# GpSimd takes over the last multiplication of the first feed-forward kind, two tiles behind its clamps

## The reference, cut to what matters

```python
cw = jnp.sum(jax.nn.one_hot(idx, E) * weights[..., None], axis=1)   # top 2 of 8 experts, per token
h1 = jnp.einsum('td,efd->etf', xt, w1) + b1[:, None, :]
h3 = jnp.einsum('td,efd->etf', xt, w3) + b3[:, None, :]
a = swiglu(h1 * h3)        # g = min(h[::2], 7), l = clip(h[1::2], -7, 7); g * sigmoid(1.702 g) * (l + 1)
y = jnp.einsum('etf,edf->etd', a, w2) + b2[:, None, :]
routed = jnp.einsum('te,etd->td', cw, y)
sh = swiglu((xt @ sw1.T + sb1) * (xt @ sw3.T + sb3))
return (routed + sh @ sw2.T + sb2).reshape(inp_shape)
```

## Time and profile before

| What | us |
|---|---|
| median of 3 runs | 1880.45 (1879.37 to 1882.93) |
| the profiled execution | 1880.12 |
| its span (first to last instruction) | 1877.9 |
| PE busy | 1719.7 (92% of the span) |
| DVE busy | 1387.3 (74%) |
| ACT busy | 906.7 (48%) |
| POOL busy | 950.4 (51%) |

### The profile page before, as it was taken

The page is one execution under the profiler, slowest core; times in us unless marked ns, Lnnn a source line. Parts: engine busy times, 40 slices in busy tenths (PEclk is TensorE's granted clock), DMA queues, the critical chain, the costliest instruction groups (busy, mean ns, idle before and its releaser), DMA issues. The chain is left out here.

```text
span 1877.9 us, 23760 instructions
## 1 busy us (share of the span) xinstructions
PE 1719.7 (92%) x7374; PEld 936.2 (50%) x7381; DVE 1387.3 (74%) x2189; ACT 906.7 (48%) x2131; POOL 950.4 (51%) x986
## 2 busy tenths in 40 slices
PE   6889988999999899979998999988898988889999
PEld 2346654555555466646665566533243333335665
DVE  5868876555555488856776677579999999997765
ACT  3335544545555355536555433556455464443332
POOL 3833332434333233432121255478989989785555
PEclk9989999999999899979998999989999999899999
DMA  6001110000000011110000133210000000002333
GB/s 246 1 17 52 52 51 12 1 1 1 1 1 1 13 46 48 55 68 1 1 2 1 63 98 103 86 34 1 17 1 13 5 6 12 1 2 81 101 97 108
DMA packets 39995, 70.37 MB, mean 37 GB/s; under 512 B 6400, under 2 KB 13696, under 8 KB 39104
## 3 DMA queue, kind: packets, MB, share of 16 engines
q1 hardware_dynamic: 39872, 68.87, 11.4%
HBM read 64.00 MB, written 1.70 MB: 35 GB/s over the span
## 5 line engine op out<-in xcount | busy, mean ns | idle before, releaser
L2138 POOL TENSOR_TENSOR ssm_hc<-ssm_h,ssm_cm 128x512 f32<-128x512 f32 x256 | 324.2, 1288 | 43.1 <-DVE ssm_h L2192 41.4
L307 PE MATMUL banks<-ffn_x_high,up_high 128*128 128x512 f32 x544 | 291.0, 535 | 8.6 <-DVE ffn_hg L920 3.9
L2077 PE MATMUL banks<-ssm_hc,const 128*128 128x512 f32 x512 | 267.4, 604 | 0.2
L2192 DVE TENSOR_TENSOR_SCAN ssm_h<-banks,ssm_dbx 128x512 f32<-128x512 f32 x208 | 249.7, 1217 | 5.8 <-issue 3.5
L2122 ACT ACTIVATE banks<-banks,a_neg 128x510 f32<-128x510 f32 x256 | 167.1, 659 | 169.3 <-PE banks L2053 167.6
L1804 POOL TENSOR_TENSOR ffn_a<-ffn_p,ffn_wide 128x512 f32<-128x512 f32 x128 | 166.3, 1301 | 142.6 <-PE banks L1736 118.5
L1527 POOL TENSOR_SCALAR wide_pin<-wide_pin,wide_rden 128x256 f32<-128x256 f32 x256 | 117.6, 478 | 221.6 <-DVE wide_rden L1545 221.6
L308 PE MATMUL banks<-ffn_x_low,up_high 128*128 128x512 f32 x544 | 216.9, 399 | 0.0
L309 PE MATMUL banks<-ffn_x_high,up_low 128*128 128x512 f32 x544 | 216.7, 398 | 0.0
L1769 ACT ACTIVATE ffn_th<-banks 128x512 f32<-128x512 f32 (+1 forms) x136 | 80.4, 597 | 181.9 <-PE banks L309 157.4
L1825 DVE SCALAR_TENSOR_TENSOR ffn_p<-ffn_th,banks 128x512 f32<-128x512 f32 (+1 forms) x136 | 93.2, 685 | 99.1 <-ACT ffn_th L1769 57.1
(11 more groups left out here) (218 smaller groups left out, 3414.9 us busy)
## 6 DMA issues: line engine op xcount, KB each, us to landing
ffn_wide<-r_kept SPq DMA_DIRECT2D x256, 128.0 KB, 2.9
ffn_wide<-r_kept SPq DMA_DIRECT2D x64, 256.0 KB, 3.1
ssm_packed<-ssm_parts SPq DMA_DIRECT2D x48, 64.0 KB, 2.0
up_whole<-in_up SPq DMA_DIRECT2D x1, 2304.0 KB, 15.3
weights<-in_weights SPq DMA_DIRECT2D x1, 2048.0 KB, 21.7
up_whole<-in_up SPq DMA_DIRECT2D x1, 2048.0 KB, 8.5
weights<-in_weights SPq DMA_DIRECT2D x1, 1168.0 KB, 23.9
weights<-in_weights SPq DMA_DIRECT2D x1, 1152.0 KB, 8.4
```

Of the source, the lines that this page charges most:

```text
L307: pe.matmul(out, w_high, x_high, start=True, stop=False)
L2077: pe.matmul(k.bank[5][:], k.c("hot")[:, P - row:2 * P - row], hc[:, i % LAG, :], start=False, stop=(i % NP == NP - 1)).then_inc(s["red"], 1)
L2138: pool.tensor_tensor(hc[:, i % LAG, :], h[:, i % HOLD, :], cm[:, i // NP % 2, :], ALU.mult) \
L2192: dve.tensor_tensor_scan(h[:, n % HOLD, :], k.bank[DELTA[n % AHEAD]][:], product, 0.0, ALU.mult, ALU.add).then_inc(s["h"], 1)
```

## The change

The last multiplication, which makes `a`, moves from DVE to POOL. A new function `weigh(g)` on POOL waits for `product` (a new semaphore that DVE counts up at line 933's place) and for the same things as before (`down` of tile g - 2, the row of `wide`). POOL calls `weigh(g - 2)` in iteration g, behind the clamps of tile g and ahead of the piece; the last two calls stand behind the loop. `p1` gets a second buffer, and DVE waits for `act` of tile g - 2 before it writes it. `a` has two buffers before and after. The counts of `act` that ACT (tanh) and SP (DMAs) wait for are unchanged, but POOL now makes them.

```diff
-        p1 = sb("ffn0_p1", [P, T])
+        p1 = sb("ffn0_p1", [P, 2, T])
...
+            def weigh(g):
+                pool.wait_ge(s["product"], g + 1)
+                if g >= 2:
+                    pool.wait_ge(s["down"], g - 1)
+                if g % N == 0:
+                    pool.tensor_scalar(a[:, g % 2, :], p1[:, g % 2, :], 0.5, None, ALU.mult).then_inc(s["act"], 1)
+                else:
+                    c = g // N * E0 + g % N - 1
+                    pool.wait_ge(s[f"cw{c % WIDE}"], 16 * (c // WIDE + 1))
+                    pool.tensor_tensor(a[:, g % 2, :], p1[:, g % 2, :], wide[:, c % WIDE, :], ALU.mult).then_inc(s["act"], 1)
+
             for g in range(ALL):
                 pool.wait_ge(s["h3"], 2 * g + 1)
                 pool.tensor_scalar(hg[:, g % 2, :], hg[:, g % 2, :], LIMIT, -BIG, ALU.min, ALU.max) \
...
                     .then_inc(s["linear"], 1)
+                if g >= 2:
+                    weigh(g - 2)
                 if g // N + 1 < PASSES:
                     gpsimd(pool, g // N + 1, g % N)
                 else:
                     follow.slot(g % N)
+            weigh(ALL - 2)
+            weigh(ALL - 1)
             follow.rest()
...
                 dve.wait_ge(s["tanh"], g + 1)
-                link(dve.scalar_tensor_tensor(p1[:], th[:, g % 2, :], 1.0, hg[:, g % 2, :], ALU.add, ALU.mult))
+                if g >= 2:
+                    dve.wait_ge(s["act"], g - 1)
+                link(dve.scalar_tensor_tensor(p1[:, g % 2, :], th[:, g % 2, :], 1.0, hg[:, g % 2, :], ALU.add, ALU.mult))
                 dve.wait_ge(s["linear"], g + 1)
-                link(dve.scalar_tensor_tensor(p1[:], hl[:, g % 2, :], 1.0, p1[:], ALU.add, ALU.mult))
+                dve.scalar_tensor_tensor(p1[:, g % 2, :], hl[:, g % 2, :], 1.0, p1[:, g % 2, :], ALU.add, ALU.mult) \
+                    .then_inc(s["product"], 1)
                 if g + 2 < ALL:
+                    dve.wait_ge(s["product"], g + 1)
                     hidden(g + 2)
-                if g >= 2:
-                    dve.wait_ge(s["down"], g - 1)
-                if g % N == 0:
-                    dve.tensor_scalar(a[:, g % 2, :], p1[:], 0.5, None, ALU.mult).then_inc(s["act"], 1)
-                else:
-                    c = g // N * E0 + g % N - 1
-                    dve.wait_ge(s[f"cw{c % WIDE}"], 16 * (c // WIDE + 1))
-                    dve.tensor_tensor(a[:, g % 2, :], p1[:], wide[:, c % WIDE, :], ALU.mult).then_inc(s["act"], 1)
-                dve.wait_ge(s["act"], g + 1)
```

More of the change, by code:

```diff
@@ L713, in biased_ffn @@
     ALL = PASSES * N
-    s = k.semaphores("ffn0", ["dve", "h", "cw0", "cw1", "h1", "h3", "gate", "linear", "tanh", "act", "down",
+    s = k.semaphores("ffn0", ["dve", "h", "cw0", "cw1", "h1", "h3", "gate", "linear", "product", "tanh", "act", "down",
                               "cw_rows", "summed", "done"] + PREP + ROUTE)
```

## The result

| What | before | changed |
|---|---|---|
| median of 4 runs, us | 1879.91 (1878.76 to 1882.93) | 1929.44 (1925.11 to 1932.90) |
| ratio to before, 95% interval | | 1.0264 (1.0249 to 1.0278) |
| profiled execution, its span, us | 1880.12, 1877.9 | 1925.11, 1923.3 |

The change costs 49.5 us where 27.6 were forecast: slower, as predicted, but 1.4 us beyond the upper end of the range.

What follows compares the result with a forecast made beforehand. PE, busy 92% of the span, was taken as the bound. Six routing passes (+15), the first run's last pass (+3) and the second run's end (+9.6) sum to +27.6 on 1880.1: 1908 us, range 1886 to 1928.

Steps and rivals of the forecast that it cites:

- PE's wait at tile 1: All eight passes: `weigh(1)` behind `x_norm` and the clamps of tile 3 makes PE's down product wait 3.7 us, 3.3 with `x_norm` undisturbed.
- The end of the second run: Second run's last passes: `weigh` lengthens POOL's list around the clearing (+2.7 us) and the rotary pieces (+6.9), +9.6 together (6 to 12).
- the routing pass: Six passes that route for a next one: each 2.5 us longer (0.4 to 5), from +0.9, 1 and 0.6; +15 us together.
- The hold of DVE: Tiles 3 to 6 of a routing pass: POOL's multiplication holds DVE 0.5 us per tile, losing 2.0 of 2.8 us won.
- What of tile 1's wait reaches DVE: Routing pass: about 1.7 of PE's 3.7 us wait reach DVE's chain, less a remnant of 0.8: +0.9 us.
- rival B: The port as bound: each POOL multiplication holds DVE 0.99 us and PE's waits of 3.7 come on top; +46, 1926 us, chance 0.18.
- Iterations 7 and 8: End of a routing pass, where DVE is behind PE: `a` comes late, costing 0 to 1.7 us, taken as 1.
- the wait of ACT: ACT's tanh of tile g waits for `weigh(g - 2)`: a ring of 5.5 to 6.5 us per two tiles, costing nothing.
- The gain side: PE's waits for `r_cw` and `hidden`: a lighter DVE list gives at most 6 x (2.2 + 0.5), about 16 us.
- A: Rival, absorbed: DVE is never held and each routing pass gives back all but 0.4 us; 1889 us, chance 0.18.
- C: Rival, faster: `weigh(1)` ends before PE reaches tile 1's down product, 16 us won, the ends cost 7; 1871 us, chance 0.08.
- D: Rival, nothing: gain and delay cancel; 1880 us, chance 0.04.

Runs made afterwards that it cites:

- e4: The kernel before with an extra scratch multiplication on POOL in every tile, for which no other engine waits; 1914.67 us, ratio 1.0190.
- e5: The kernel before with an extra scratch memset on POOL in every tile, which only writes and for which no other engine waits; 1880.09 us, ratio 1.0004.
- e7: The changed kernel with POOL's multiplications one tile behind its clamps instead of two, for all tiles; 1866.50 us, ratio 0.9933 to the kernel before.
- e10: The changed kernel with POOL's multiplication ahead of the clamps, not behind them, still two tiles behind; 1879.29 us, ratio 0.9995 to the kernel before.
- e8: The changed kernel with 15 unused short products on PE in front of each pass's tile 1 down product; 1919.52 us, ratio 1.0214 to the kernel before.
- e9: The changed kernel with ACT's tanh waiting for DVE's product of tile g - 2, not for POOL's multiplication; 1918.82 us, ratio 1.0212 to the kernel before.
- e3: The kernel before with DVE's multiplication for `a` cut to 32 of 512 columns and nothing added to POOL; 1852.22 us, ratio 0.9851.
- e1: The changed kernel with only tile 1's multiplication issued earlier, in iteration 2 ahead of `x_norm`; 1907.43 us, ratio 1.0146 to the kernel before.

## Why the prediction was right and wrong

**Right.** PE's wait at tile 1: forecast 3.3 if `x_norm` is undisturbed, measured 3.54 in the pass shown, and a wait at all eight tiles 1 (3.5 in the six routing passes, 1.5 and 3.2 in the two last ones). The last pass of the first run: +3 forecast, +4.4 measured. The end of the second run: +9.6 forecast, +11.6 measured. The chain that was written down is there, `rot_q`, `rot_k` and what stands behind them in POOL's list: from `rot_k` to the bias product (844) it is 11.7 us before and 15.7 after, 4.0 more where 4.2 + 0.7 were forecast. That the whole is near is partly luck. Of the 9.6, 2.7 stood for the clearing, which falls in the pass before (a wait of 1.33 at 819.25); that leaves 6.9 for the last pass against 11.6, and its wait at tile 1, 3.16, stands in no term of the forecast. The one wait of 7 us behind `rot_q` came as two of 4.86. PE's rows in the changed kernel, against the earlier trace rows:

```profile
847.81 2.08 PE L840 MATMUL banks<-ffn_a,weights 128*128 128x512 f32 x2 [4.86 <-POOL ffn_a L905]
...
864.03 2.08 PE L840 MATMUL banks<-ffn_a,weights 128*128 128x512 f32 x2 [4.86 <-POOL ffn_a L905]
...
871.76 3.96 PE L840 MATMUL banks<-ffn_a,weights 128*128 128x512 f32 x4 [0.93 <-POOL ffn_a L905]
```

**Wrong: the routing pass, 2.5 us forecast and 6.4 measured, 23 us over six.** This is the step that failed; it has three terms.

- *The hold of DVE* is the step that was mis-sized most. I took 0.5 us per tile, 2.0 of the 2.8 won, plus 0.6 for the small operations, on the ground that `hidden` would cover half of the multiplication. The trace has 4.75 - 0.33 = 4.4 us over the four tiles, 1.1 each: more than the upper bound of 0.99 once the small operations are counted. The bound came from one long row; the mistake was the cover. `weigh` stands behind the clamps, the clamps stand behind `hidden`, so when `weigh` starts `hidden` is over, and the multiplication falls on 950 and on the routing operations behind it. That could have been read from the order of the two lists beforehand. Instead of 0.2 us shorter (-0.8 + 0.6) DVE's stretch became 2.2 longer, which is also why the wait for `r_cw` stayed at 1.9 and gave nothing back. e4 against e5 shows the mechanism, e7 and e10 that the cover was to be had by moving `weigh`.
- *What of tile 1's wait reaches DVE*: 1.7 forecast, 3.0 measured on the mean. The mechanism by itself is a little smaller than forecast: in the one later pass whose clock stayed up after the same wait (738 us, granted 1.00) the part from 322 to `hidden` is 11.3, 1.4 over before. In the three others of its kind it is 12.9, another 1.6, with the clock down. In the first pass of each run a wait of 1.8 us for tile 0's `a` (901) is added. The prediction named the clock under rival B without a price; e8 takes 10 us of it back.
- *Iterations 7 and 8*: 1 forecast, 1.1 measured as the rest of the pass. From the routing product to the bias product at the end of the pass (844) the kernel before takes 9.6 us where the clock stays up and 11.0 to 11.2 where it falls behind the wait for `r_cw`; the changed kernel takes 11.1 to 11.2 in either case (12.8 in the pass with the clearing), since with the clock up PE waits 1.24 us for `a` there instead (719.85). So the late `a` that was forecast is there, with 1.5 us, and half of the passes before had lost that much already by the clock.

**Wrong: the wait of ACT, of which the prediction says that it costs nothing.** The ring of tanh, 948, 950, `hidden`, clamps and `weigh` was put at 3.25 us a tile and under PE's 3.67. The working was also too low by its own numbers: 6.5 us allows 0.5 for each of the two holds, and with the 0.99 that the range used the ring is 7.5 us, or 3.7 a tile, which leaves no slack. At tile 1 it isn't the ring that counts but the one late `weigh(1)`, for which a tanh of ACT waits 1.6 us (237.42), and DVE's 948 after it. e9 puts it at 10.6 us of the total. e8's and e9's gains may share a part, since both shorten what follows tile 1; they weren't tried together.

**The gain side** was too small as well: 16 us was called the most, e3 shows 27.6. The changed kernel kept none of it, since its DVE stretch got longer.

**The rivals.** B, the port as bound, with 1926, came nearest: its wait of 3.7 on top of a DVE as late as before is what the trace shows, with DVE 2.2 later than that. A is refuted: DVE's operations are longer. C said what is worth having, `weigh(1)` done before PE wants it, at 1871; the changed order doesn't give it, e7's does, at 1868. D is refuted with A.

**Left open.** How the 49.5 us divide between order and hold: e1 takes 22 away by the order of one tile, e4 gives 35 for the hold and the clock behind it, and they overlap. Nor was it tried what makes the same wait end with the clock lowered in one pass and not in another.

## What to carry to other kernels

When work goes from DVE to GpSimd, lay the two lists side by side and see what DVE executes in the microseconds in which GpSimd will read SBUF: beside DVE operations with a PSUM operand neither engine was held (e7, 0.7% faster than before), beside those with two SBUF operands both were (the change, 2.6% slower, with tile 1 behind `x_norm` as well). Where an in-order list puts a result behind a piece that itself waits for something, look at the consumer of that one tile, and count a possible lowered clock with each long wait of PE behind which PE sets the pace.

## What the runs showed of the hardware

- Reading decides, not occupation: 1.24 us of reading per tile on POOL cost 35 us (e4), 1.27 us of writing nothing that could be measured (e5, ratio 1.0004).
- The hold works in both directions and chains: `weigh` 1.26 to 1.69 us by what runs on DVE, 950 0.69 to 1.67. A 128x32 operation of 0.19 us can take 1.10.
- The granted clock fell to about 0.57 and 0.62 of full speed in the microseconds after waits of 3.5 and 1.9 us. Its price was 1.6 us where PE set the pace behind the wait, and about nothing where PE had to wait for `a` anyway. The kernel before has the same, after some of its equal waits of 2.2 us for `r_cw` and not after others, which makes the difference between its passes of 42.2 and of 40.6 us:

```profile
731.70:735.00 3.30, 3.23 (x8) 1.87 (x9) 3.23 (x6) 1.06 (x2) 1.01 (x2) 0.50 0.14 36
...
773.97:777.00 3.03, 3.03 (x14) 2.17 (x15) 2.96 (x5) 1.75 (x3) 0.81 (x2) 1.00 0.18 43
```
